# Token sums of a mixture layer as half-row products: 64 rows by 256 columns in place of 128 by 512

## The reference

```python
x = x + gnn(layernorm(x), ...)              # graph layer: edges, two dense layers with batch norm
x = x + ffn(layernorm(x)[None], ...)[0]     # the mixture, where the change is

def ffn(x, controller, f1, f2):             # x: 10000 tokens of 512; groups of 16 tokens
    grouped = x.reshape(B, S // 16, 16, D)
    cont_logits = einsum('bgtd,des->bgtes', grouped, controller) + tie     # e: 16, s: 4
    cont_perm = (cont_logits == max(cont_logits over t))                   # 0 or 1
    intermediate = einsum('bgtd,desf->bgtesf', grouped, f1)
    inner = relu(einsum('bgtesf,bgtes->bgesf', intermediate, cont_perm))   # f: 32
    inter2 = einsum('bgesf,esfd->bgesd', inner, f2)
    result = einsum('bgesd,bgtes->bgtd', inter2, cont_perm)
```

## Time and profile before

| | |
|---|---|
| median of 3 runs | 2142.18 us (2140.15 to 2145.62) |
| the profiled execution | 2146.73 us, span 2145.0 us |
| TensorE busy | 1937.7 us (90%), 15080 products |
| VectorE busy | 1210.1 us (56%) |
| ScalarE busy | 1005.3 us (47%) |
| GpSimd busy | 387.9 us (18%) |

### The profile page before, as it was taken

How to read it: one execution, slowest core, us unless ns; L and a number is a source line. 1 busy time by engine, 2 the same in 40 slices (tenths; PEclk the granted TensorE clock), 3 DMA queues, 4 the chain that set the end, 5 groups by cost and what they waited for, 6 DMA issues and landing times. The chain is left out here.

```text
span 2145.0 us, 40442 instructions
## 1 busy us (share of the span) xinstructions
PE 1937.7 (90%) x15080; PEld 1389.2 (65%) x15080; DVE 1210.1 (56%) x2533; ACT 1005.3 (47%) x1742; POOL 387.9 (18%) x481
## 2 busy tenths in 40 slices
PE   0777399999999899999999589999999999999987
PEld 0233278888888678888888456666666666666653
DVE  1456256656666444333333457677676776767754
ACT  0454123333332276565655256555565555655542
POOL 1577230000000000000000332222222222222200
PEclk9898699999999999999999799999999999999999
DMA  9887746656665434343432464343343433434311
GB/s 376 215 150 127 151 116 195 180 156 180 185 170 157 148 141 167 115 172 115 169 117 100 166 208 138 105 135 110 110 137 106 134 109 110 138 105 134 99 56 64
DMA packets 182810, 309.08 MB, mean 144 GB/s; under 512 B 33065, under 2 KB 107305, under 8 KB 179594
## 3 DMA queue, kind: packets, MB, share of 16 engines
q1 hardware_dynamic: 169674, 285.35, 42.5%
q0 software_dynamic: 8960, 20.98, 5.1%
q10 hardware_dynamic: 4032, 0.80, 0.2%
HBM read 172.20 MB, written 134.87 MB: 143 GB/s over the span
## 5 line engine op out<-in xcount | busy, mean ns | idle before, releaser
L1392 PE MATMUL bank<-f2s,inner_bd 128*32 128x512 f32 x2560 | 301.2, 601 | 2.7 <-issue 1.6
L1296 ACT ACTIVATE inter_hi<-bank 128x512 fp32r<-128x512 f32 x320 | 191.3, 598 | 195.7 <-PE bank L1392 193.4
L1227 DVE TENSOR_TENSOR inter_lo<-bank,inter_hi 128x512 fp32r<-128x512 f32 x320 | 220.8, 690 | 94.5 <-ACT inter_hi L1296 94.4
L419 PE MATMUL bank<-ahi,w_hi 128*128 128x500 f32 x640 | 250.8, 392 | 14.4 <-DVE alo L760 14.4
L606 ACT ACTIVATE h1o<-bank,b_by_channel 128x500 f32<-128x500 f32 x160 | 108.5, 678 | 328.2 <-PE bank L421 328.2
L419 PE MATMUL bank<-hhi,w_hi 128*128 128x500 f32 x640 | 252.0, 394 | 2.5 <-DVE hlo L567 2.5
L421 PE MATMUL bank<-hhi,w_lo 128*128 128x500 f32 x640 | 250.2, 391 | 0.0
L420 PE MATMUL bank<-hlo,w_hi 128*128 128x500 f32 x640 | 249.7, 390 | 0.0
L420 PE MATMUL bank<-alo,w_hi 128*128 128x500 f32 x640 | 249.3, 389 | 0.0
L421 PE MATMUL bank<-ahi,w_lo 128*128 128x500 f32 x640 | 248.9, 389 | 0.0
L1276 ACT ACTIVATE yT<-bank 128x512 f32<-128x512 f32 x320 | 173.7, 597 | 84.3 <-PE bank L1366 83.4
(11 more groups left out here) (124 smaller groups left out, 3274.0 us busy)
## 6 DMA issues: line engine op xcount, KB each, us to landing
h1T<-h1o SPq DMA_DIRECT2D x19, 2000.0 KB, 8.1
h1in<-h1T SPq DMA_DIRECT2D x19, 2000.0 KB, 9.6
aggregate<-zeros SPq DMA_DIRECT2D x20, 1024.0 KB, 8.3
h2in<-h2T SPq DMA_DIRECT2D x40, 512.0 KB, 4.0
x<-in_x SPq DMA_DIRECT2D x80, 256.0 KB, 2.7
x<-x SPq DMA_DIRECT2D x80, 256.0 KB, 3.8
x_back<-x SPq DMA_DIRECT2D x80, 256.0 KB, 3.1
out<-x_back SPq DMA_DIRECT2D x80, 256.0 KB, 2.0
```

Source lines behind the costliest of these rows:

```text
L419: nc.tensor.matmul(out, w_hi[:, k, cols], a_hi[:, k, :], start=(k == 0), stop=False)
L1227: nc.vector.tensor_tensor(ilo[u % QB][:, :], bI[u % QB][:, :], ihi[u % QB][:, :].bitcast(F32), ALU.subtract).then_inc(ilr, 1)
L1296: nc.scalar.activation(ihi[n % QB][:, :], bI[n % QB][:, :], ACT.Copy).then_inc(ihr, 1)
L1392: last = nc.tensor.matmul(bI[b][32 * i:32 * i + 32, :], ibd[:, e, j, :, :].rearrange("p s g -> p (s g)"), f2s[:, e, :], start=True, stop=True)
```

## The change

It is described as sums over tokens in one run of 32 half-row products: four groups a row half, the second half of the chunks into two of the intermediate product's banks.

The tile's 8 groups lie four in rows 0 to 63 and four in rows 64 to 127. `perm_bd` now has 4 group columns per pair (`GH = 4`), so 256 columns; row half 0 reads them as groups 0 to 3, row half 1 as groups 4 to 7, and the mask compares with the group number modulo 4. Each chunk is done in two row halves of 64 rows, each with `xn2_hi` and `xn2_lo`, 256 columns: 16 calls a tile. The row halves write to different banks: chunks 0 and 1 to banks 2 (half 0) and 3 (half 1), chunks 2 and 3 to banks 4 and 5, which units 0 and 1 use. `sum_a` and `sum_b` become one step `sums` in the place of `sum_a` (in the first tile of a block both were adjacent already), so `logits`, and in steady tiles `rows`, follow the whole run. TensorE waits, ahead of the run, for all copies of the tile before, in its middle for `inter_lo` of unit 1, and ahead of units 0 and 1 for the copies of the last sums. ScalarE copies four times 512 elements as before, each time two chunks of one row half, in runs of 4 and not 8.

```diff
@@ mixture
-        pbd = sb("perm_bd", [P, ES, GB], F32R)
+        pbd = sb("perm_bd", [P, ES, GH], F32R)
+        bY = [bD, bI[0:2]]
@@ schedule, steady tile
                     if front is not None:
-                        yield "sum_a", m
+                        yield "sums", m
                     yield "rows", m
                     if next_:
                         yield "logits", m + 1
-                    if front is not None:
-                        yield "sum_b", m
@@ vector
-                nc.vector.tensor_scalar(pq[:, 0:1], pidx[:, :], 4, None, ALU.logical_shift_right).then_inc(cstv, 1)
+                nc.vector.tensor_scalar(pq[:, 0:1], pidx[:, :], 4, GH - 1, ALU.logical_shift_right, ALU.bitwise_and).then_inc(cstv, 1)
...
-                    nc.vector.tensor_tensor(pbd[:, :, :], bP.unsqueeze(2).to_broadcast([P, ES, GB]),
-                                            mtg[:, :].unsqueeze(1).to_broadcast([P, ES, GB]), ALU.mult).then_inc(pbr, 1)
+                    nc.vector.tensor_tensor(pbd[:, :, :], bP.unsqueeze(2).to_broadcast([P, ES, GH]),
+                                            mtg[:, :].unsqueeze(1).to_broadcast([P, ES, GH]), ALU.mult).then_inc(pbr, 1)
@@ scalar
-                def to_yT(k, j, c):
+                def to_yT(k, j, c, r):
                     t = k * TB + j
-                    act.wait_ge(yp, t * KH + c + 1)
-                    nc.scalar.activation(yT[:, c, :, j * GB:(j + 1) * GB],
-                                         bD[c % 2][:, :].rearrange("p (e g) -> p e g", g=GB), ACT.Copy).then_inc(yr, 1)
+                    act.wait_ge(yp, t * KH + c + r + 1)
+                    nc.scalar.activation(yT[:, c:c + 2, :, j * GB + r * GH:j * GB + (r + 1) * GH],
+                                         bY[c // 2][r][:, :].rearrange("p (c e g) -> p c e g", c=2, g=GH), ACT.Copy).then_inc(yr, 1)
@@ tensor
-                def sums(k, j, chunks):
+                def sums(k, kb, j):
...
+                    if not static(t, 1):
+                        pe.wait_ge(yr, t * KH)
+                    for h in range(2):
+                        if h and kb is not None:
+                            pe.wait_ge(ilr, unit_of(kb, j * QB + 1) + 1)
+                        done = {}
+                        for c in (2 * h, 2 * h + 1):
+                            for part in (xhi, xlo):
+                                for r in range(2):
+                                    rows = slice(r * HP, (r + 1) * HP)
+                                    done[r] = nc.tensor.matmul(
+                                        bY[h][r][:, (c % 2) * HP * GH:(c % 2 + 1) * HP * GH],
+                                        part[j % 2][rows, c * P:(c + 1) * P],
+                                        pbd[rows, :, :].rearrange("p e g -> p (e g)"), start=part is xhi, stop=part is xlo)
+                        for r in range(2):
+                            done[r].then_inc(yp, 1)
...
-                def inter(kb, u):
+                def inter(k, kb, u):
                     j, b, q = u // QB, u % QB, unit_of(kb, u)
+                    if b < 2:
+
+                        pe.wait_ge(yr, (k * TB + j if k is not None else NB * TB) * KH)
```

More of the change, by code:

```diff
@@ L38 @@
 QB = ES // GT
+GH = GB // 2
+HP = P // 2
 UB = 3
@@ L870, in mixture @@
         gid, tgid = sb("gid", [P, GB]), x1b[1][:, 0:P]
-        mtg, mrt = sb("mask_token_group", [P, GB]), sb("mask_row_token", [P, P])
+        mtg, mrt = sb("mask_token_group", [P, GH]), sb("mask_row_token", [P, P])
         bA, bB, bD, bI = psum[0], psum[1], psum[2:4], psum[4:8]
+        bY = [bD, bI[0:2]]
         bL, bP = bB[:, 0:P], bB[:, 0:ES]
@@ L1161, in _ @@
                 dve.wait_ge(cstv, GT + 6)
-                nc.vector.tensor_scalar(mtg[:, :], gid[:, :], pqf[:, 0:1], None, ALU.is_equal).then_inc(cstv, 1)
+                nc.vector.tensor_scalar(mtg[:, :], gid[:, 0:GH], pqf[:, 0:1], None, ALU.is_equal).then_inc(cstv, 1)
                 nc.vector.tensor_scalar(mrt[:, :], tgid[:, :], pqf[:, 1:2], None, ALU.is_equal).then_inc(cstv, 1)
@@ L1282, in body @@
                             nonlinear(k, *n)
-                        if what == "sum_a":
+                        if what == "sums":
                             if n == 0 and not static(k, 1):
                                 act.wait_ge(inp, k * QB)
[L1286 to L1290, removed]
+                            for c in range(0, KH, 2):
+                                for r in range(2):
+                                    to_yT(k, n, c, r)
                         if what == "unit":
@@ L1348, in turn_p @@
                     nc.tensor.matmul(bP, pn[j % 2][:, :], eye[:, :], start=True, stop=True).then_inc(ptp, 1)
-                def sums(k, j, chunks):
+                def sums(k, kb, j):
                     t = k * TB + j
[L1353 to L1366, removed]
+                    pe.wait_ge(pbr, t + 1)
+                    pe.wait_ge(xlr, t + 1)
+                    if j == 0 and not static(k, 1):
+                        pe.wait_ge(inv, k * QB * 2)
+                        pe.wait_ge(ina, k * QB * 2)
+                    if not static(t, 1):
[12 more added lines that the diff above has]
+                                        pbd[rows, :, :].rearrange("p e g -> p (e g)"), start=part is xhi, stop=part is xlo)
+                        for r in range(2):
+                            done[r].then_inc(yp, 1)
                 def rows(k, kb, j):
@@ L1434, in body @@
                             turn_p(k, n)
[L1435 to L1438, removed]
+                        if what == "sums":
+                            sums(k, kb, n)
                         if what == "rows":
@@ L1441, in body @@
                         if what == "unit":
-                            inter(kb, n)
+                            inter(k, kb, n)
                         if what == "final":
```

## The result

| | before | after |
|---|---|---|
| median of the runs | 2143.9 us (4 runs) | 2117.17 us (4 runs, 2114.0 to 2118.97) |
| span of the profiled execution | 2145.0 us | 2116.9 us |
| TensorE busy | 1937.7 us, 15080 products | 1907.6 us, 15720 products |
| VectorE busy | 1210.1 us | 1193.9 us |

The ratio is 0.9882, with a 95% interval of 0.9865 to 0.9899: the change takes 1.2% of the time away. Run again beside the last experiment it gave 0.9865 (0.9847 to 0.9882).

What follows compares the result with a forecast made beforehand. TensorE was taken to bound the steady tiles; 20.2 us there and 11.3 in first tiles off the profiled 2146.73 gave 2115.2, or 2110.7 as median of the runs. Its own range was 2102 to 2121, for 8 in 10 2098 to 2174.

Steps and rivals of the forecast that it cites:

- The pairs: In the sums' run, each tile's sixteen half-row products were to overlap two by two, 0.94 us against 1.88 before.
- The change of shape: In a steady tile, changing the array's shape into and out of the half-row run was to cost 0.47 us.
- What is late next: In 63 steady tiles, `final` would wait for VectorE's `back_bd`, leaving 0.32 us won each, 20.2 us in all.
- Rival 3: In steady tiles, no other engine comes last and the whole 0.47 us is won: 2101 us, chance 0.06.
- First tiles: In the 9 first tiles of a block, the sums were to take 1.26 us less each, 11.3 us in all.
- First block: In the 8 tiles of the first block alone, small terms of both signs: 0, with 3 us either way.
- The edits at nothing: Across the tiles, the smaller `perm_bd`, yT copies in runs of 4 and new TensorE waits were to cost nothing.
- The total: Over the whole kernel, 20.2 + 11.3 = 31.5 us off the profiled execution's 2146.73 us.

Runs made afterwards that it cites:

- the last experiment: The first new order, with VectorE's select ahead of the new tile's statistics and the normalisation behind the result in steady tiles: ratio 0.9806 to the kernel before, median 2101.27 us.
- the second experiment: The changed kernel with all eight half-row products of rows 0 to 63 first, then those of rows 64 to 127: ratio 1.0063 to the kernel before.
- the first new order: The changed kernel with `rows` right behind unit 3 and `turn_g` behind the sums in steady tiles: ratio 0.9826 to the kernel before, steady tiles 9.48 us.

## Why the prediction was right, and where it was off

- **The pairs.** Taken at 0.94 us by the nearest rows, those of the strips; measured eight pairs at 0.12, the two of a pair starting within 0.01 us of each other, and the second experiment shows the price without them. Each product has a load of its own: 0.111 us for a load and 0.117 for half a full product would be 0.228 one behind the other, and the pairs are 0.118 us apart. In the second experiment one half alone goes at 0.12 as well, with loads and products on the same rows. The rule of the Trainium skill that spoke against it (TensorE: Matmul & The Clock Gate, "Part 3: Packing small matmuls — row/col tiling": loads overlap products only of another row group) does not hold in these traces.
- **The change of shape.** I took 0.47 us for in and out. The run's 1.16 us less eight pairs of 0.118 leaves 0.22; ahead of it the last transposes take 0.53 us to the next product for 0.36 before, and behind it `rows` take 0.50 for 0.39; a run of full rows has 0.08 of this too, its first load laid bare. Together that is 0.42, and the experiment with two runs gives 0.40. The step is right and its size was about a sixth too high. It had no effect on the sum, because `back_bd` came last anyway.
- **What is late next.** This was the step that mattered: 0.32 us a steady tile and not all that TensorE saves. Measured 0.31 in the tile shown and 0.30 in the mean over 54 (16.4 / 54), with `final` starting 0.05 to 0.06 us after `back_bd` in each. Rival 3, the whole gain, was out for the reason given.
- **What I had missed.** `rows` stand behind the whole run now, so `back_bd` has a second path, from `rows` on. In the changed kernel it is 0.12 us shorter than the one through the statistics, so the sum stood; it is the one that comes last in the kernels with full rows and with short statistics, and it upset two later expectations (9.69 and 9.11 for 9.79 and 9.26). The expectations for the two new orders take the 0.10 us for a cost of TensorE's own and name TensorE alone; the starts of `final` show a wait for VectorE in both.
- **First tiles.** 11.3 us forecast, 11.8 between the spans. The run's 1.15 us and the 0.13 that `final` takes more are the 1.28 of the forecast, so 1.26 less in that piece of each; with the expert stages ahead of it eight of the tiles are 0.98 shorter. That the total over the nine agrees so well is luck in part, since 3.9 us of it come from the first of these tiles, where a stop moved across the border to the first block.
- **First block.** Put at 0 with 3 us either way, measured +3.0. The stop of 3.8 us is more than all of it: without it the eight tiles would be 0.8 us shorter.
- **The edits at nothing.** `perm_bd` 415 ns (0.42 forecast), copies to yT 601 ns in the median with runs of 4 elements (597 before, the mean), unit 0 never waits for them.
- **The total.** 31.5 us forecast; 28.1 between the spans, of which +1.3 lie ahead of the mixture; 1.2% by the ratio, where the forecast was 1.5%. The difference is for the most part the first block and that start.

## What to carry to other kernels

A product whose contraction is block diagonal can be cut into row halves with half the columns each; issued alternately, here into different banks, they ran in pairs, and 1.88 us of products became 0.94. Keep all of them in one run: each change of the array's shape and back cost 0.40 us here. Before counting such a saving, look for the wait that ends next (here a VectorE result with 0.47 us to spare), and when it is moved out of the way, look again: the first new order only put another wait in its place, and the second is still held by one. Look for it in the starts (a product that follows a VectorE result by 0.05 us in every tile), since the chain of waits did not name it.

## What the runs showed of the hardware that I had not expected

- Products of the second row half don't have to be issued alternately to overlap: with eight of one half queued ahead of them, they started alongside the last four (1654.73 against 1655.09 for the first half's last). How far ahead this reaches in general no run here tells.
- In an expert stage TensorE stops now and then with no releaser in the profile. In the trace of before there are 22 such stops (two of its products by f1 over 0.4 us apart), and ahead of each the last 16 KB packet of DMA queue q8, kind "instruction" on the page, ends 1.24 to 1.60 us before TensorE goes on; of after it is 21 of 21, 1.27 to 1.66 us. That TensorE waits there for its instructions is a reading of these times; most packets of that queue stand beside no stop, and no run changes the transfer alone. The page of after has 101 such packets for 95, with 640 products more and a load for each.
- The granted clock differs between kernels in the last block (0.92 before, 0.91 after, 1.00 with short statistics and with either new order), and is worth some 3 to 4 us of a difference between two spans.
- The stored x came back later in the changed kernel (3.6 us from issue to landing in the median, for 3.1): VectorE's `result` waited for that transfer 25 times, 27.9 us in all, against 3 times and 4.0 us before, and steady tiles did not get longer for it.
